# A graph network, two transformer layers and experts in one kernel: the order of the experts' tail, and epsilon as a column beside z

## The reference, cut to what matters

```python
def _L0_ffn_ref(x, router_w, w1, b1, w2, b2, gamma, beta):   # x: layernorm of the stream, 1024 x 512; E, F = 8, 32
    logits = xf @ router_w
    gate_vals, idx = jax.lax.top_k(logits, 2)
    gates = jax.nn.softmax(gate_vals, axis=-1)
    for e in range(E):
        h = jax.nn.relu(xf @ w1[e] + b1[e]) @ w2[e] + b2[e]
        y = _layernorm(xf + h, gamma[e], beta[e])            # EPS = 1e-06
        w = jnp.sum(jnp.where(idx == e, gates, 0.0), axis=-1)
        out = out + w[:, None] * y
    return out                                               # the caller adds it to x
```

## Time and profile before

| | us |
|---|---|
| median of 3 runs | 1143.89 |
| lowest and highest run | 1142.52, 1146.07 |
| the profiled execution | 1144.43 |
| its span, from first to last instruction | 1142.5 |
| TensorE matmuls busy | 1086.5 (95%) |
| VectorE busy | 706.8 (62%) |
| ScalarE busy | 365.4 (32%) |
| GpSimd busy | 148.9 (13%) |

### The profile page before, as it was taken

One profiled execution on the slowest core, in us unless ns is written; L12 is line 12 of the kernel. 1 busy time (PEld: TensorE's weight loads), 2 busy tenths in 40 slices (PEclk: granted clock), 3 DMA queues, 4 the chain that ended last, 5 costly groups with the idle time before them and its releaser, 6 DMA issues.

```text
span 1142.5 us, 16284 instructions
## 1 busy us (share of the span) xinstructions
PE 1086.5 (95%) x6080; PEld 887.3 (78%) x6080; DVE 706.8 (62%) x1530; ACT 365.4 (32%) x671; POOL 148.9 (13%) x141
## 2 busy tenths in 40 slices
PE   7999899999999999999899999999999999999995
PEld 6767799878777777777798888777777888787763
DVE  7576677378766567465666469675563215834586
ACT  4335466525321211135466515221210002011231
POOL 4230202000000000300202000000000802200027
PEclk9999999999999999999999999999999999999998
DMA  6220101002222112000101003212156201100001
GB/s 212 111 93 1 38 1 39 1 5 83 82 53 78 53 50 79 1 1 1 38 2 38 1 5 97 88 48 64 56 193 229 94 20 38 36 1 1 1 10 65
DMA packets 34655, 60.17 MB, mean 53 GB/s; under 512 B 19441, under 2 KB 20401, under 8 KB 33937
## 3 DMA queue, kind: packets, MB, share of 16 engines
q1 hardware_dynamic: 12688, 41.21, 11.0%
q10 hardware_dynamic: 21888, 17.87, 4.9%
HBM read 48.59 MB, written 10.49 MB: 52 GB/s over the span
## 4 chain that ended last, share of the span: by engine, by line
PE 77%; DVE 10%; ACT 5%; issue 4%; POOL 3%; DMA 0%; POOLq 0%; ACTq 0%; DVEq 0%
PE ps_a L528 10%; PE ps_a L530 10%; PE ps_a L529 10%; PE ps_v L528 9%; PE ps_v L530 8%; PE ps_v L529 8%; PE ps_a L905 5%; PE ps_v L741 5%; PE ps_a L549 2%; PE ps_a L671 2%; PE ps_v L752 2%; ACT work L1090 2%; DVE expk L1556 2%; ACT expk L1051 1%; PE ps_v L625 1%
## 5 line engine op out<-in xcount | busy, mean ns | idle before, releaser
L528 PE MATMUL ps_a<-ht_hi,w_hi 128*128 128x512 f32 x488 | 193.7, 397 | 2.7 <-DVE w_lo L1822 0.9
L530 PE MATMUL ps_a<-ht_hi,w_lo 128*128 128x512 f32 x488 | 191.6, 393 | 0.0
L529 PE MATMUL ps_a<-ht_lo,w_hi 128*128 128x512 f32 x488 | 191.3, 392 | 0.0
L1001 ACT ACTIVATE work<-ps_a,col_sb 128x512 f32<-128x512 f32 x96 | 66.4, 719 | 198.7 <-PE ps_a L530 143.3
L528 PEld LDWEIGHTS ps_a<-ht_hi,w_hi 128*128 128x128 f32 x488 | 92.3, 189 | 25.7 <-DVE headmask_r L1521 1.3
L1675 DVE TENSOR_TENSOR xm<-ps_v,xm 128x512 f32<-128x512 f32 x80 | 55.2, 691 | 86.0 <-PE ps_v L530 85.3
L530 PEld LDWEIGHTS ps_a<-ht_hi,w_lo 128*128 128x128 f32 x488 | 92.3, 189 | 19.9
L529 PEld LDWEIGHTS ps_a<-ht_lo,w_hi 128*128 128x128 f32 x488 | 92.3, 189 | 19.3
L528 PE MATMUL ps_v<-w_hi,f_hi 128*128 128x512 f32 x256 | 101.7, 397 | 0.0
L530 PE MATMUL ps_v<-w_hi,f_lo 128*128 128x512 f32 x256 | 99.7, 389 | 0.0
L529 PE MATMUL ps_v<-w_lo,f_hi 128*128 128x512 f32 x256 | 99.6, 389 | 0.0
(11 more groups left out here) (240 smaller groups left out, 2016.8 us busy)
## 6 DMA issues: line engine op xcount, KB each, us to landing
stage<-wstream SPq DMA_DIRECT2D x62, 512.0 KB, 3.6
adj_d<-adj_win ACTq DMA_DIRECT2D x16, 256.0 KB, 2.9
adj<-adj_d ACTq DMA_DIRECT2D x2, 2048.0 KB, 11.9
xt_d<-xt_hi SPq DMA_DIRECT2D x2, 1024.0 KB, 5.0
xt_d<-xt_lo SPq DMA_DIRECT2D x1, 2048.0 KB, 11.4
ht_hi<-xt_d ACTq DMA_DIRECT2D x1, 2048.0 KB, 8.7
ht_lo<-xt_d ACTq DMA_DIRECT2D x1, 2048.0 KB, 13.4
x_again<-x ACTq DMA_DIRECT2D x8, 256.0 KB, 9.0
```

The lines of the kernel that those rows point to most:

```text
L528: nc.tensor.matmul(ps, left[0], right[0], start=first, stop=False)
L529: nc.tensor.matmul(ps, left[0], right[1], start=False, stop=False)
L530: return nc.tensor.matmul(ps, left[1], right[0], start=False, stop=last)
L1001: nc.scalar.activation(work[:, n % 4, :], psA[:, i % BANKS, :], func, **how).then_inc(a_empty, 1)
```

## The change

- **Epsilon as a column.** The buffers of z get a 513th column, set once to sqrt(EPS x 512) by two VectorE memsets. ScalarE squares 513 columns, each number scaled by 1/sqrt(512), so that the sum holds the mean square and epsilon. GpSimd's addition of epsilon is taken out, with its semaphore. The squares themselves, which nobody reads, go to buffers of their own, and hm, z and weighted move by 32 bytes to make room. `add_z` of the second half waits for the weighing that read the same buffer.
- **Orders of the second half.** In ring V z of tile 2 comes ahead of the logits and those ahead of tile 0's scales. TensorE makes the second product of tile 1 ahead of the transposes, the two of tile 2 around the logits' product, the scale products of tile 0 behind the turned logits, and tile 3's first product behind the turned choice. From tile 4 on the scale products run three tiles behind z. VectorE adds z of tiles 1 and 2 and makes the choice before it weighs tile 0, and from tile 4 on weighs three tiles behind z. ScalarE squares tile 1 ahead of the logits.
- **GpSimd.** The first addition waits for VectorE's low parts of the hidden layer (h1_split at 4). Scales of tiles 6 and 7 both come ahead of the additions of tiles 5 and 6, and tile 7's come in one call.

```diff
--- before.py
+++ after.py
@@ -224,8 +224,8 @@
 )
 TAIL_V = numbered(
     [("lin", t) for t in range(4)] + [("logits", 0)] + [("lin", t) for t in range(4, NT)]
-    + both_z(0) + both_z(1) + scales(0) + [("logits", 1)]
-    + [name for t in range(2, NT) for name in both_z(t)]
+    + both_z(0) + both_z(1) + both_z(2) + [("logits", 1)] + scales(0)
+    + [name for t in range(3, NT) for name in both_z(t)]
 )
 
 
@@ -360,15 +360,18 @@
...
-        hm = [[at(f"hm{q}_{h}", [P, 2, 2, 512], f32r, region, skip * KB) for h, (region, skip) in enumerate(places)]
-              for q, places in enumerate(((("v", 0), ("v", 8)), (("k", 8), ("slots", 40))))]
+        SIDE = 32
+        hm = [[at(f"hm{q}_{h}", [P, 2, 2, 512], f32r, region, skip) for h, (region, skip) in enumerate(places)]
+              for q, places in enumerate(((("v", 0), ("v", 8 * KB)), (("k", 8 * KB), ("slots", 40 * KB - SIDE))))]
         hotT = at("hot_t", [3 * SET, N], f32r, "nat")
         hot = at("hot", [P, NT, 3 * SET], f32, "hots", 8 * KB)
         logit2 = at("logit2", [P, NT, 2 * EXP], f32, "nat", 7 * KB)
         logit_t = at("logit_t", [2 * EXP, N], f32, "nat", 8 * KB)
-        zz = [at(f"z{q}", [P, HALF_NT, D], f32, "slots", 16 * KB + 32 * KB * q) for q in range(2)]
-        weighted = [at(f"weighted{n}", [P, 2, D], f32, region, skip * KB)
-                    for n, (region, skip) in enumerate((("slots", 8), ("slots", 12), ("nat", 12), ("work", 4)))]
+        zz = [at(f"z{q}", [P, HALF_NT, D + 1], f32, "slots", (16 + 32 * q) * KB - SIDE) for q in range(2)]
+        squares = [at(f"squares{n}", [P, D + 1], f32, region, skip) for n, (region, skip) in enumerate((("work", 0), ("nat", 4 * KB)))]
+        weighted = [at(f"weighted{n}", [P, 2, D], f32, region, skip)
+                    for n, (region, skip) in enumerate((("slots", 8 * KB - SIDE), ("slots", 12 * KB - SIDE), ("nat", 12 * KB),
+                                                        ("work", 4 * KB)))]
 
 
         psA = ctx.enter_context(nc.psum_tensor("ps_a", [P, BANKS, 512], f32))
@@ -406,7 +409,7 @@
...
-        square_eps, square_root, scale_ready = sem("square_eps"), sem("square_root"), sem("scale_ready")
+        eps_beside, square_root, scale_ready = sem("eps_beside"), sem("square_root"), sem("scale_ready")
...
@@ -955,34 +958,28 @@
             second_layer(1, 0)
             second_bias(1)
             second_layer(0, 1)
+            second_layer(1, 1)
             turn_experts_input(1)
-            second_layer(1, 1)
+            second_bias(2)
+            second_layer(0, 2)
             route(1)
+            second_layer(1, 2)
+            turn_logits(1)
             pick_scales(0)
-            turn_logits(1)
             hidden(1, 0)
             hidden(1, 1)
-            second_bias(2)
-            second_layer(0, 2)
             turn_hots(1)
-            second_layer(1, 2)
-            spread_hots(1)
             second_bias(3)
             second_layer(0, 3)
+            spread_hots(1)
             second_layer(1, 3)
-            second_bias(4)
-            pick_scales(1)
-            second_layer(0, 4)
-            pick_scales(2)
-            second_layer(1, 4)
-            for t in range(HALF_NT + 1, NT):
+            for t in range(HALF_NT, NT):
                 second_bias(t)
-                pick_scales(t - 2)
+                pick_scales(t - 3)
                 second_layer(0, t)
-                if t == NT - 1:
-                    pick_scales(NT - 2)
                 second_layer(1, t)
-            pick_scales(NT - 1)
+            for t in range(NT - 3, NT):
+                pick_scales(t)
 
 
         @block.scalar
@@ -1224,7 +1221,8 @@
                     column = slice(n, n + 1)
                     if n >= 2:
                         act.wait_ge(squared, n - 1)
-                    nc.scalar.activation(work[:, n % 2, :], zz[q][:, t % HALF_NT, :], ACT.Square, scale=D ** -0.5,
+                    act.wait_ge(eps_beside, q + 1)
+                    nc.scalar.activation(squares[n % 2][:], zz[q][:, t % HALF_NT, :], ACT.Square, scale=D ** -0.5,
                                          accum_out=square_mean[:, column]).then_inc(squared, 1)
 
             for m in range(KT):
@@ -1241,8 +1239,8 @@
             take_hots(0)
             high_turned(1)
             square(0)
+            square(1)
             take_logits(1)
-            square(1)
             raise_gates(1)
             take_hidden(1, 0)
             take_hidden(1, 1)
@@ -1377,9 +1375,6 @@
 
                 columns = slice(2 * t + first, 2 * t + last)
                 pool.wait_ge(squared, 2 * t + last)
-                nc.gpsimd.tensor_scalar(square_mean[:, columns], square_mean[:, columns], EPS_MOE, None,
-                                        ALU.add).then_inc(square_eps, last - first)
-                pool.wait_ge(square_eps, 2 * t + last)
                 nc.gpsimd.tensor_tensor(gscale[:, columns], square_mean[:, columns], nhalf[:, columns],
                                         ALU.pow).then_inc(square_root, last - first)
                 pool.wait_ge(square_root, 2 * t + last)
@@ -1398,17 +1393,20 @@
                 nc.gpsimd.tensor_tensor(Xm[:, t, :], Xm[:, t, :], weighted[t % 4][:, 0, :], ALU.add).then_inc(summed, 1)
 
             pool.wait_ge(hots_ready, 1)
-            for t in range(NT - 1):
+            for t in range(NT - 2):
                 if t == HALF_NT:
                     pool.wait_ge(hots_ready, 2)
                 scale(t, 0, 2)
                 if t:
+                    if t == 1:
+                        pool.wait_ge(h1_split, 4)
                     add_pair(t - 1)
                     add_experts(t - 1)
-            scale(NT - 1, 0, 1)
-            add_pair(NT - 2)
-            scale(NT - 1, 1, 2)
-            add_experts(NT - 2)
+            for t in range(NT - 2, NT):
+                scale(t, 0, 2)
+            for t in range(NT - 3, NT - 1):
+                add_pair(t)
+                add_experts(t)
 
 
         @block.vector
@@ -1922,7 +1920,9 @@
 
             def add_z(q, t):
                 h, n = divmod(t, HALF_NT)
-                nc.vector.tensor_tensor(zz[q][:, n, :], tail_job("z", q, t), Xf[h][:, n, :], ALU.add).then_inc(v_empty, 1)
+                if h:
+                    (taken_v if ("gamma", q, n) in TAIL_V else taken_a)(dve, "gamma", q, n)
+                nc.vector.tensor_tensor(zz[q][:, n, 0:D], tail_job("z", q, t), Xf[h][:, n, :], ALU.add).then_inc(v_empty, 1)
 
             def scale_job(name):
                 dve.wait_ge(*((v_full, TV + TAIL_V[name] + 1) if name in TAIL_V else (a_full, TA + TAIL_A[name] + 1)))
@@ -1932,7 +1932,7 @@
                 name, column = ("gamma", q, t), slice(2 * t + q, 2 * t + q + 1)
                 ps = scale_job(name)
                 dve.wait_ge(scale_ready, 2 * t + q + 1)
-                nc.vector.scalar_tensor_tensor(out=weighted[t % 4][:, q, :], in0=zz[q][:, t % HALF_NT, :],
+                nc.vector.scalar_tensor_tensor(out=weighted[t % 4][:, q, :], in0=zz[q][:, t % HALF_NT, 0:D],
                                                scalar=gscale[:, column], in1=ps, op0=ALU.mult,
                                                op1=ALU.mult).then_inc(scale_empty(name), 1)
 
@@ -1968,34 +1968,30 @@
             onto_graph(6)
             mask_hidden(0, 1)
             onto_graph(7)
+            for q in range(2):
+                nc.vector.memset(zz[q][:, :, D:D + 1], (EPS_MOE * D) ** 0.5).then_inc(eps_beside, 1)
             add_z(0, 0)
             normalise_experts(1)
             add_z(1, 0)
             add_z(0, 1)
+            add_z(1, 1)
             low_turned(1)
-            add_z(1, 1)
+            add_z(0, 2)
+            add_z(1, 2)
+            choose(1)
             take_scales(0)
-            choose(1)
             low_hidden(1)
-            add_z(0, 2)
             mask_hidden(1, 0)
-            add_z(1, 2)
+            add_z(0, 3)
             mask_hidden(1, 1)
-            add_z(0, 3)
             add_z(1, 3)
-            take_scales(1)
-            add_z(0, 4)
-            take_scales(2)
-            add_z(1, 4)
-            for t in range(HALF_NT + 1, NT - 1):
-                take_scales(t - 2)
+            for t in range(HALF_NT, NT):
+                take_scales(t - 3)
                 add_z(0, t)
                 add_z(1, t)
-            take_scales(NT - 3)
+            for t in range(NT - 3, NT - 1):
+                take_scales(t)
             last = NT - 1
-            add_z(0, last)
-            take_scales(last - 1)
-            add_z(1, last)
             add_shift(last)
             dve.wait_ge(summed, last - 3)
             for q in range(2):
```

## The result

| | before | changed | ratio, 95% interval |
|---|---|---|---|
| median of 20 runs each | 1144.76 us | 1141.45 us | 0.9963 [0.9949, 0.9977] |
| span of the profiled execution | 1142.5 | 1139.4 | |

One of the 20 runs of the changed kernel took 1235.33 us at a granted clock of 0.845 and is left out of the ratio. The two medians are 3.3 apart; the interval of the ratio is a gain of 2.6 to 5.8 us; the forecast was 2.8.

The account below looks back on a forecast made before the run. GpSimd's chain in the experts' tail bounds the kernel: S 1114.78 plus 24.95 (chain 22.05, then 0.4 and 2.5 for the last store and end) gives span 1139.7, 2.8 under 1142.5; median forecast 1141.1 us, range 1139.3 to 1143.3.

Parts of the forecast that it names:

- S: Start of GpSimd's pair sum of tile 1, when its weighted pair is ready; put at 1114.78, 0.32 us earlier.
- chain: GpSimd's work after S, additions of tiles 1 to 6 and scales of tiles 3 to 7; put at 22.05 us.
- The turns: VectorE's last two additions and GpSimd's additions of tiles 5 and 6 exclude each other over SBUF; cost 0.7 us.
- Rival A: At the end, VectorE's two additions fall between GpSimd's and cost nothing; gain 3.5 us, 1140.4; chance 0.18.
- The faster choice is hidden: VectorE's choice gains 1.6 us without GpSimd's additions beside it, but TensorE has no use for it before 1103.98.
- The wait for the low parts: GpSimd's first addition held back from 1098.91 to 1106.2; nothing of this reaches S.
- the 2.96 of the chain: GpSimd's saving after S, 24.31 to 21.35 us: 1.44 from four epsilons, 1.53 from tile 7's scales in one call.
- TensorE's margin: TensorE's period of 3.6 us a tile against GpSimd's 3.75: thin, 0.15 a tile, but entering some 2 us ahead.
- rival D: GpSimd no longer the limit, TensorE or the scale's way is; about 1 us gained or nothing, 1142.9 or 1143.9; chance 0.11.
- a sign of being wrong: In the changed kernel's profile, the chain that ended last running through TensorE or ScalarE after 1116.
- Rival B: S moves back by about 1 us, as mask products hang on a new chain; gain 1.5, 1142.4; chance 0.17.
- C: Rows of 513 numbers slow each operation on z; at 0.3 us each, 3.7 us slower, 1147.6; chance 0.05.

Follow-up runs that it names:

- e4: Changed kernel, with VectorE's two weighings of tile 7 written back into PSUM; 0.9980 [0.9963, 0.9998], 52.98 us from statistics to end against 53.85.
- e7: Changed kernel with two more VectorE additions (results unused) ahead of the choice; 54.43 us from the second half's statistics to the end, against 53.85.
- r4: Same kernel as e7, run again; 0.9976 [0.9960, 0.9993] against the kernel before, 54.40 us from the second half's statistics to the end.
- e3: Changed kernel without GpSimd's new wait for the low parts; 54.49 us from the second half's statistics to the end, against 53.85.
- e1: Kernel before with the epsilon column alone, all orders as before; 0.9972 [0.9948, 0.9996], 54.03 us from statistics to end against 56.79 before.
- r1: Changed kernel unaltered, run again; 0.9968 [0.9950, 0.9986] against the kernel before, 54.35 us from statistics to end against 53.85 in its first profile.

## Why the prediction was right, and where it was not

**The end by GpSimd's chain: right.** S + chain + store gave 1139.7; the span is 1139.4. Luck has a part in that: the three terms were off by 0.05, -0.64 and 0.26. S was put at 1114.78 and is 1114.83, but 0.16 of that is the earlier statistics: from them on it is 29.28, where I had 29.07. The step that slipped is the mask products (20.84, not 20.63): the biases of tile 3 start 0.52 behind the turned choice, not 0.36, and the hidden products take 5.61, not 5.57 (24 at 0.23 and 0.1 are 5.62). The start of the hidden products was put at 1098.41, 12.70 after the statistics, and is 12.72, but the terms named for it (1097.2, 0.68 and 0.43) give only 1098.31. The chain was put at 22.05 and is 21.41: the step into a scale was mis-sized, since the power starts 1.23 to 1.26 behind the sum where I kept epsilon's 1.37. That is 0.12 for each of four tiles, and again about 0.15 ahead of tile 6's pair sum. From GpSimd's end to the span's end it is 3.16, where I had 2.9.

**The turns: right**, and what kept the tail's gain under 3. Put at 0.7, measured 0.8 to 0.87 (e4). Rival A fell: neither of VectorE's additions found a gap.

**The faster choice is hidden: right** (e7 and r4). **The wait for the low parts** doesn't lengthen anything and saves 0.15 (e3).

**Where the 2.96 of the chain come from: half wrong.** I gave 1.44 to epsilon and 1.53 to making tile 7's scales in one call ahead of the additions. But those two calls held two epsilons, which the column takes out as well, and the shorter step I did not have. e1 has the same chain (21.55) without the new order at the end. What the one call saves (0.78 + 1.22 against 0.99) the turns take back but for 0.14 (chains of 21.55 and 21.41), since the additions of tiles 5 and 6 now run beside VectorE's last two. Without the turns the chain lost 3.70 (24.31 to 20.61, in e4) where I had 2.96, with them 2.90 where I had 2.26, and I credited half of it to the wrong edit: the column carries 2.76 of the 2.94.

**The other engines: right about the mean, too easy about the margin.** I named TensorE's margin thin, 0.15 a tile from 3.6 against 3.75, and then gave rival D 0.11. The periods are 3.65 and 3.63: the margin a tile is nothing, and only the head start is left. With the full clock TensorE and VectorE stay ahead. With the low clock, in five profiles of ten, D does happen where GpSimd has the short chain (four of them), at tile 2, and costs 0.5, not 2. The prediction named as a sign of being wrong a chain that ended last through TensorE or ScalarE after 1116. In r1 that sign is there (TensorE until 1123.90), and it is rival D at work. In the first profile of the changed kernel the profile's chain also passes through ScalarE's squares of tile 5 until 1119.86; but GpSimd has no idle time from 1114.83 on and takes that tile's power only at 1124.72, so those squares held up nothing. Rival B was 0.2 instead of 1, and C didn't happen: z is still 0.69 and the weighing 0.74 on rows of 513.

**The measured ratio** is at 3.7 to 4.2 us, above the 2.9 of the tails, with intervals that hold both; no profile shows where more than the 2.9 would come from. That the median came to 1141.45 where I had 1141.1 is luck in part as well: I started from the 1143.89 of three runs, the 20 runs of the kernel before have 1144.76, 0.87 more, and the medians lie 3.3 apart, 0.5 more than I had. I gave 0.30 to more than 0.3%; the measurement has its centre there and its interval reaches to either side.

## What to carry to other kernels

In a chain on the slowest engine, count small operations by the distance between starts: an epsilon of 0.22 us cost 0.48 a tile, and folding it into a reduction that ran anyway was worth more than all the reordering around it. When a reordering puts two engines side by side at the end, look at which operands both read from SBUF before counting the gain. Where whole executions differ by more than the change is worth, count from an operation ahead of the edit to the end; here such distances agreed to 0.05 us for the same kernel at the same granted clock, while the start of the tail differed by 6.6 between profiles. And take more than one profile of a kernel: the second of the changed kernel showed a low clock that the first did not, worth 0.5.

## What the runs showed of the hardware

- A GpSimd power behind a 512-column sum starts 1.26 after it, the addition of epsilon 1.37 after it (1117.47 - 1116.21 and the earlier trace rows).
- GpSimd and VectorE with two SBUF operands take turns both ways: VectorE's additions 1.28 and 0.98 instead of 0.69, GpSimd's 1.71 and 1.59 instead of 1.26 (changed kernel against e4), and the low part 1.77 instead of 0.69 (e3 against the changed kernel).
- TensorE's granted clock fell to 0.53, the 1.2 GHz level, right behind waits of 0.28 and 1.23 us, in five of ten profiles with the same products there, and the products stood 0.43 apart instead of 0.23 (rows of r1).
- VectorE and ScalarE work on rows 2052 bytes apart, 32 bytes off, at their usual speed (in the changed kernel z 0.69, weighing 0.74, squares 0.64; before 0.69, 0.75 and 0.63).
